# A new order of all five instruction lists in an attention and expert feed-forward kernel

## The chip, the cores and the metric

The kernel runs on one core of one Trainium2 chip. Its time is the device time of one execution in microseconds (us), smaller is better. A core has five engines, each working through its own list of instructions: TensorE (PE; its weight loads are shown as PEld), VectorE (DVE), ScalarE (ACT), GpSimd (POOL) and SyncE (SP), which here only issues transfers. ScalarE issues a few transfers too.

## The reference

For 8 batches of 128 rows and 256 columns, in float32: normalise x, attend over the 256 columns of the context in 8 heads of width 16, add; normalise again, and put each row through one of two experts (256 to 1024 to 256, a squared leaky ReLU between), chosen by a router; add.

```python
def reference(x, ctx_2048, itok_B_779_1933, L0_ffn_w_router, L0_ffn_w_fc, L0_ffn_w_proj):
    x = x + _L0_xcond_ref(_layernorm(x, axis=-1), ctx_2048, ctx_2048, itok_B_779_1933)
    x = x + _L0_ffn_ref(_layernorm(x, axis=-1), L0_ffn_w_router, L0_ffn_w_fc, L0_ffn_w_proj)
    return x
# attention
    s = SCALE * jnp.log(k_length.astype(jnp.float32))[:, None, None, None]
    attn = jnp.einsum('bhdq,bhdk->bhqk', qh, kh)
    attn = jax.nn.softmax(s * attn, axis=-1)
    out = jnp.einsum('bhqk,bhdk->bhdq', attn, vh)
# experts
    h = jnp.einsum('nd,ehd->enh', x_flat, w_fc)
    a = jnp.square(jnp.where(h >= 0, h, 0.5 * h))
    expert_out = jnp.einsum('enh,edh->end', a, w_proj)
    out = jnp.einsum('end,en->nd', expert_out, mask * top_weight[None, :])
```

## The kernel before

Every matmul of the reference is done as a sum of products of high and low parts: a float32 operand is split into a rounded part (`_hi`, a copy on ScalarE into the type fp32r) and the rest (`_lo`, a subtraction on VectorE or GpSimd), and hi*hi, hi*lo and lo*hi are added in PSUM.

The work is cut into 8 batches (b) for the attention and 4 groups of two batches (g) for the feed-forward. Each engine has a list of calls written out by hand; the order of the list is the order of execution on that engine. Between engines, semaphores are counted: a call waits until the counters that it needs have reached a value, and everything behind it on its engine waits with it.

Attention of one batch. x is loaded (`load_x`), its mean and variance are taken (`x_moments`, three stages, VectorE), the inverse root is found on ScalarE (`x_ln`, `x_rstd`) and refined (`x_newton`), and q is normalised (`q_normalise`) and split (`q_part_hi`, `q_part_lo`). The keys are loaded (`load_kv`) and split (`k_part_hi`, `split_k`). Six transfers from SBUF to SBUF spread q and k over the partitions so that the three products lie in one contraction (`stack_q`, `stack_k`, 128 KB each); for q of batch 0 TensorE does it instead (`q_permute`, with the selection `sel` that GpSimd builds from the constants, and `q_put`). `scores_qk(b, g)` computes the scores with queries on partitions, four g per batch, only to find the row maxima (`row_max`, VectorE). The maxima are split (`split_max_hi`, `split_max_lo`), turned (`max_transpose`, TensorE) and copied (`max_rows`, ScalarE). `scores_kq(b, g)` computes the scores with keys on partitions and the maximum taken off; for b below 4 the maximum comes in by extra matmuls with `pick`, for later ones through a stack (`stack_max`, with `clear_max` and `stack_pick` before it). `exp(b, g)` on ScalarE gives the weights, with a scale that needs `len_scale`. `values(b, 0)` and `values(b, 1)` multiply by the values (`load_v`, `place_v`), 16 matmuls of 32 columns each. VectorE turns and divides the result (`pv_turn`, `den_inverse`, `attention_out`, `attention_turn`) and adds x (`keep`, `x2_sum`).

Feed-forward of one group. `x2_moments`, `y_ln`, `y_rstd`, `x2_newton`, `x2_normalise` normalise; `x_transpose(g)` turns both batches on TensorE and `xt_part_hi`, `xt_part_lo` split them. `ffn1(g, c)` is 6 matmuls for 128 hidden units, c from 0 to 15; for two c at a time `leaky` and `square_hi` (ScalarE), `square` (GpSimd) and `square_lo` (VectorE) give the high and low part, and `ffn2(g, c)` is 6 matmuls that add up the output of an expert. `router`, `coef_*`, `coefs` and `expert_out` weight and add, `store` writes. The weights come in 16 pieces of 256 KB (`load_weights(0, n)` for w_fc, `(1, n)` for w_proj), each split by `split_w` on ScalarE and then on GpSimd or, for w_proj, `split_w_lo` on VectorE.

`warm(k)` and `fill(n)` are matmuls of zeros (two matmul records each) that give TensorE something to do.

TensorE works in four shapes: 128 rows by 128 columns (ffn1, ffn2, x_transpose, zeros, max_transpose up to batch 3), 64 rows (both scores), 32 columns (values), and 128 by 32 for max_transpose from batch 4 on.

Two lines set what waits on the maxima and on the scores of a batch:

```python
wait(pe, s_max, PAIRS * b + (g - sets + 1))          # scores_qk: sets = 2 for b < 2, else 1
wait(pe, s_exp, PAIRS * b + g - (1 if b == 1 and g > 0 else 0))   # scores_kq
```

## Time and profile before

| | before |
|---|---|
| median of 3 runs | 173.63 us (172.86 to 173.75) |
| span of the profiled execution | 170.4 us |
| TensorE busy | 161.4 us (95%) |
| VectorE busy | 129.2 us (76%) |
| ScalarE busy | 97.0 us (57%) |
| GpSimd busy | 58.6 us (34%) |
| bytes moved by DMA | 16.98 MB |

The span runs from the first to the last instruction of one profiled execution; the time of a run has what surrounds the program on top. A busy time is an average over stages with different limits, and a matmul's end is modelled, so that TensorE can be shown busy while it runs below its pace: the step from one matmul's start to the next tells more.

### The profile page before, as it was taken

What the parts mean: (1) busy time and instruction counts of PE and PEld (TensorE: products, weight loads), DVE (VectorE), ACT (ScalarE), POOL (GpSimd) and SP (SyncE); (2) the same over time, 40 slices, a digit from 0 to 9 for tenths busy, and PEclk for the clock granted to TensorE, in tenths of its full rate; (3) what the DMA queues carried; (4) which work ended last, traced back from release to release, by engine and by line L of the source; (5) the groups of instructions that cost most, each with busy time, mean ns of one, the idle gap of its engine ahead of it and who ended that gap; (6) DMA issues with size and microseconds to landing.
All of it is one profiled execution on the core that took longest, in us unless ns stands there. A gap on an engine that the chain in (4) does not pass through costs nothing.

```text
span 170.4 us, 4075 instructions
## 1 busy us (share of the span) xinstructions
PE 161.4 (95%) x1494; PEld 139.9 (82%) x1494; DVE 129.2 (76%) x301; ACT 97.0 (57%) x181; POOL 58.6 (34%) x68
## 2 busy tenths in 40 slices
PE   7998887899999989999989999999999999999992
PEld 7986745487698869896978798969879999999991
DVE  7799987999898999995999867953179875056442
ACT  4444979558659956957346526943794065335220
POOL 7331544630322420372521260405023253136330
PEclk9999999999999999999999999999999999999999
DMA  4577857794468054004501460002010000010001
GB/s 120 167 241 246 259 190 233 217 292 126 143 229 251 3 161 120 14 19 139 174 0 62 125 189 4 0 0 67 0 62 0 4 0 0 4 61 0 0 4 62
DMA packets 18883, 16.98 MB, mean 100 GB/s; under 512 B 1776, under 2 KB 18672, under 8 KB 18864
## 3 DMA queue, kind: packets, MB, share of 16 engines
q1 hardware_dynamic: 18144, 16.00, 30.3%
q10 hardware_dynamic: 720, 0.73, 1.5%
q8 instruction: 12, 0.20, 0.5%
q14 instruction: 7, 0.06, 0.1%
HBM read 8.72 MB, written 1.05 MB: 57 GB/s over the span
## 4 chain that ended last, share of the span: by engine, by line
PE 75%; DVE 11%; issue 4%; SPq 3%; ACT 3%; DMA 2%; DVEq 0%; ACTq 0%
PE hp L1358 25%; PE ops L1388 22%; PE pv L1342 6%; PE stp L1318 6%; PE ops L1273 5%; DVE negm L813 5%; PE snp L1265 3%; DMA x_raw<-x 2%; ACT probs L514 2%; DVE a_lo L921 2%; PE ops L1376 2%; PE pv L1376 1%; PE stp L1324 1%; PE pv L1398 1%; PE snp L1301 1%
## 5 line engine op out<-in xcount | busy, mean ns | idle before, releaser
L378 POOL TENSOR_TENSOR a_buf<-l_buf 128x512 f32<-128x512 f32 x32 | 35.7, 1119 | 77.8 <-DVE a_lo L921 44.6
L514 ACT ACTIVATE probs<-stp,scale_b 128x1024 f32<-128x1024 f32 x30 | 33.4, 1114 | 14.8 <-PE stp L1318 11.3
L1358 PE MATMUL hp<-xt_hi,wfc_hi 128*128 128x256 f32 x128 | 37.2, 291 | 0.0
L813 DVE TENSOR_REDUCE negm<-snp 128x4 f32<-128x1024 f32 x28 | 34.1, 1218 | 3.6 <-PE snp L1265 3.4
L1358 PE MATMUL hp<-xt_hi,wfc_lo 128*128 128x256 f32 x128 | 35.8, 279 | 0.0
L1358 PE MATMUL hp<-xt_lo,wfc_hi 128*128 128x256 f32 x128 | 35.7, 279 | 0.0
L522 ACT ACTIVATE l_buf<-hp 128x512 f32<-128x512 f32 x32 | 18.8, 594 | 23.7 <-PE hp L1358 17.0
L921 DVE TENSOR_TENSOR a_lo<-a_buf,a_hi 128x512 fp32r<-128x512 f32 x32 | 26.2, 831 | 7.6 <-ACT a_hi L529 6.2
L1358 PEld LDWEIGHTS hp<-xt_hi,wfc_hi 128*128 128x128 f32 x128 | 24.0, 188 | 2.1 <-issue 1.0
L1388 PE MATMUL ops<-wproj_hi,a_hi 128*128 128x256 f32 x112 | 23.6, 292 | 0.5 <-DVE wproj_lo L953 0.5
L1358 PEld LDWEIGHTS hp<-xt_hi,wfc_lo 128*128 128x128 f32 x128 | 24.1, 188 | 0.0
L1358 PEld LDWEIGHTS hp<-xt_lo,wfc_hi 128*128 128x128 f32 x128 | 24.1, 188 | 0.0
L1388 PE MATMUL ops<-wproj_hi,a_lo 128*128 128x256 f32 x112 | 22.3, 281 | 0.0
L1388 PE MATMUL ops<-wproj_lo,a_hi 128*128 128x256 f32 x112 | 22.3, 281 | 0.0
L529 ACT ACTIVATE a_hi<-l_buf 128x512 fp32r<-128x512 f32 x32 | 19.7, 625 | 2.2 <-PE ops L1388 2.1
L1388 PEld LDWEIGHTS ops<-wproj_hi,a_hi 128*128 128x128 f32 x112 | 17.1, 188 | 2.1 <-issue 1.1
L1273 PE MATMUL ops<-blank 128*128 128x128 f32 x100 | 17.0, 321 | 1.1 <-DVE blank L808 1.1
L1388 PEld LDWEIGHTS ops<-wproj_hi,a_lo 128*128 128x128 f32 x112 | 17.2, 188 | 0.0
L1388 PEld LDWEIGHTS ops<-wproj_lo,a_hi 128*128 128x128 f32 x112 | 17.2, 188 | 0.0
L1318 PE MATMUL stp<-q_st,k_st 64*128 64x256 f32 x120 | 16.1, 319 | 1.0 <-ACT probs L514 0.8
L1273 PEld LDWEIGHTS ops<-blank 128*128 128x128 f32 x100 | 14.7, 224 | 2.7 <-DVE blank L808 1.1
L1342 PE MATMUL pv<-probs,v_one 128*32 128x256 f32 x256 | 16.8, 385 | 0.0
(112 smaller groups left out, 237.2 us busy)
## 6 DMA issues: line engine op xcount, KB each, us to landing
k_st<-k_hi SPq DMA_DIRECT2D x16, 128.0 KB, 2.1
wfc_raw<-w_fc_t SPq DMA_DIRECT2D x8, 256.0 KB, 4.4
wproj_raw<-w_proj_t SPq DMA_DIRECT2D x8, 256.0 KB, 3.5
q_st<-q_hi SPq DMA_DIRECT2D x14, 128.0 KB, 2.1
x_raw<-x SPq DMA_DIRECT2D x8, 128.0 KB, 3.0
k_st<-k_lo SPq DMA_DIRECT2D x8, 128.0 KB, 2.4
v_raw<-ctx_t SPq DMA_DIRECT2D x8, 128.0 KB, 2.6
x_keep<-x SPq DMA_DIRECT2D x8, 128.0 KB, 2.7
```

Of the source, the lines that this page charges most:

```text
L378: pool.tensor_tensor(a_buf[d % 2][:, :, :], l_buf[d % 2][:, :, :], l_buf[d % 2][:, :, :], ALU.mult).then_inc(s_a, 1)
L514: act.activation(probs[g][:, :, :, :], pair[:, :, :].rearrange("p e (c n) -> p e c n", c=KC), ACT.Exp, scale=scale_b[:, b:b + 1]).then_inc ...
L522: act.activation(l_buf[d % 2][:, :, :], hp[:, d % 2, :].rearrange("p (c n) -> p c n", c=2), ACT.Prelu, alpha=0.5).then_inc(s_l, 1)
L529: act.activation(a_hi[d % NA][:, :, :], l_buf[d % 2][:, :, :], ACT.Square).then_inc(s_ahi, 1)
L813: dve.tensor_reduce(negm[b % 2][:, :, :, g].rearrange("p c e -> p e c"), pair[:, :, :].rearrange("p e (c n) -> p e c n", c=KC), AX.X, ALU. ...
L921: dve.tensor_tensor(a_lo[d % NA][:, :, :], a_buf[d % 2][:, :, :], a_hi[d % NA][:, :, :].bitcast(f32), ALU.subtract).then_inc(s_alo, 1)
L1265: last = pe.matmul(pair[:, e, qc * KEYS:(qc + 1) * KEYS], q_st[j][rows, g, qc * P:(qc + 1) * P], k_st[j][rows, g, :], start=(qc == 0), sto ...
L1273: pe.matmul(ops_[:, 0:P], blank[:, :], blank[:, :], start=True, stop=True, skip_group_check=True)
L1318: last = pe.matmul(pair[:, e, kc * DIM:(kc + 1) * DIM], k_st[j][rows, g, kc * P:(kc + 1) * P], q_st[j][rows, g, :], start=(kc == 0), stop= ...
L1342: last = pe.matmul(pv[32 * g:32 * g + 32, e * DIM:(e + 1) * DIM], v_one[j][:, kc * HEADS + h, :], probs[h // 2][:, h % 2, kc, :], start=(e ...
L1358: last = pe.matmul(hp[:, d % 2, half], wfc[w][:, kc, c * P:(c + 1) * P], xt[:, kc, :], start=(c % 2 == 0 and kc == 0 and w == 0 and xt is ...
L1388: last = pe.matmul(ops_[:, t * DIM:(t + 1) * DIM], a[d % NA][:, c % 2, t * P:(t + 1) * P], wproj[w][:, c, :], start=(c % CH == 0 and part ...
```

## The change

All five lists are written in a new order. No call is added or dropped, and no call is changed. On SyncE the first two weight pieces go ahead of the first stacks, and x, keep, v and kv loads and weight pieces are placed between the stacks of one batch and the next instead of among them. On ScalarE the constants are issued ahead of the first keys, and several `split_w` go earlier. On VectorE the moments of x of batches 6 and 7, `x2_normalise` and `q_part_lo` move, as do the low parts of w_proj. On GpSimd `fill_v`, `make_zeros`, `split_k` and `place_v` move. On TensorE the zeros are spread differently, scores and feed-forward calls are interleaved differently, and `values(b, 0)` and `values(b, 1)` are set apart by other calls from batch 2 on. In the core of the diff the heading of each part names the engine's list.

```diff
# SyncE
             load_x(sp, 0)
             load_x(sp, 1)
+            load_weights(sp, 0, 0)
+            load_weights(sp, 0, 1)
             stack_k(sp, 0, 0)
             stack_k(sp, 0, 1)
             stack_k(sp, 0, 2)
+            load_v(1)
             load_x(sp, 2)
-            load_kv(sp, 2)
-            load_weights(sp, 0, 0)
-            load_v(0)
+            load_weights(sp, 0, 2)
+            load_weights(sp, 0, 3)
+            keep(1)
+            load_x(sp, 3)
             stack_k(sp, 1, 0)
             stack_k(sp, 1, 1)
+            stack_k(sp, 1, 2)
             stack_q(sp, 1, 0)
             stack_q(sp, 1, 1)
-            load_x(sp, 3)
-            stack_k(sp, 1, 2)
             stack_q(sp, 1, 2)
-            load_weights(sp, 0, 1)
-            keep(0)
-            load_weights(sp, 0, 2)
-            load_weights(sp, 0, 3)
+            load_v(0)
...
# GpSimd
 
+            fill_v(0)
             zero_k(0)
             zero_k(1)
             zero_nm(0)
             zero_nm(1)
-            fill_v(0)
-            fill_v(1)
-            make_zeros()
             fill_sel(0)
             fill_sel(1)
             split_k(1)
             split_w(0, 0)
+            split_w(0, 1)
+            split_w(0, 2)
             place_v(0)
             split_k(2)
-            split_w(0, 1)
-            split_w(0, 2)
+            fill_v(1)
+            place_v(1)
             split_w(0, 3)
             split_k(3)
-            place_v(1)
+            split_k(4)
             split_w(0, 4)
             split_w(0, 5)
+            place_v(2)
+            place_v(3)
             split_w(0, 6)
-            place_v(2)
             split_w(0, 7)
-            place_v(3)
-            split_k(4)
             square(0, 0)
             square(0, 1)
+            split_k(5)
             square(0, 2)
             square(0, 3)
-            split_k(5)
             square(0, 4)
             square(0, 5)
+            make_zeros()
             place_v(4)
+            place_v(5)
+            split_k(6)
+            split_k(7)
             square(0, 6)
-            split_k(6)
             square(0, 7)
-            place_v(5)
-            split_k(7)
             square(1, 0)
+            square(1, 1)
             place_v(6)
-            square(1, 1)
+            place_v(7)
             square(1, 2)
             square(1, 3)
# ScalarE
 
-            act.preload_act_table_set("natural_log_exp_and_others")
+            act.preload_act_table_set('natural_log_exp_and_others')
+            load_consts()
             load_kv(act, 0)
-            load_consts()
             load_kv(act, 1)
             k_part_hi(0)
             x_ln(0)
             x_rstd(0)
-            q_part_hi(0)
             x_ln(1)
             x_rstd(1)
-            k_part_hi(1)
+            q_part_hi(0)
+            pick_rows()
...
             x_rstd(2)
+            x_ln(3)
+            x_rstd(3)
             exp(0, 0)
-            x_ln(3)
-            split_w(0, 1)
-            x_rstd(3)
             exp(0, 1)
+            k_part_hi(2)
+            k_part_hi(3)
+            exp(0, 2)
+            exp(0, 3)
...
# VectorE
             x_moments(0, 0)
             x_moments(0, 1)
             x_moments(0, 2)
+            len_float()
             split_first_k()
+            x_moments(1, 0)
             x_newton(0, 0)
+            x_moments(1, 1)
             x_newton(0, 1)
+            x_moments(1, 2)
             q_normalise(0)
-            x_moments(1, 0)
-            x_moments(1, 1)
-            x_moments(1, 2)
             q_part_lo(0)
-            len_float()
             x_newton(1, 0)
             x_newton(1, 1)
+            q_normalise(1)
             q_put()
-            q_normalise(1)
+            q_part_lo(1)
             row_max(0, 0)
-            q_part_lo(1)
             row_max(0, 1)
             row_max(0, 2)
             row_max(0, 3)
...
             row_max(1, 3)
-            x_moments(4, 1)
+            x_moments(5, 0)
+            q_part_lo(2)
             split_max_hi(1)
-            q_part_lo(2)
+            x_newton(4, 0)
             split_max_lo(1)
-            x_moments(4, 2)
+            x_newton(4, 1)
+            x_moments(5, 1)
+            x_moments(5, 2)
             pv_turn(0)
...
+            x2_moments(0, 1)
             row_max(2, 1)
-            x2_moments(0, 1)
-            x_moments(6, 0)
             x2_moments(0, 2)
-            x_moments(6, 1)
             row_max(2, 2)
...
             row_max(3, 0)
+            x_newton(5, 1)
+            x2_newton(0, 1)
             x2_newton(1, 0)
+            x2_normalise(0)
             x2_newton(1, 1)
+            row_max(3, 1)
             x2_normalise(1)
-            row_max(3, 1)
-            x_newton(5, 0)
+            q_part_lo(4)
+            row_max(3, 2)
             xt_part_lo(0)
-            x_newton(5, 1)
...
-            router_diff()
+            row_max(3, 3)
+            split_max_hi(3)
+            router(0)
+            split_max_lo(3)
+            split_w_lo(1, 0)
+            x_moments(6, 0)
             q_normalise(5)
-            row_max(3, 2)
-            q_part_lo(4)
...
+            x2_moments(2, 0)
+            split_max_hi(4)
+            split_max_lo(4)
+            square_lo(0, 1)
             x_moments(7, 0)
             x_moments(7, 1)
-            square_lo(0, 0)
...
-            pv_turn(3)
-            q_part_lo(5)
-            coefs(0)
             den_inverse(3)
             attention_out(3)
...
+            x2_normalise(2)
+            x2_normalise(3)
+            split_w_lo(1, 4)
+            coefs(0)
+            row_max(5, 0)
+            square_lo(0, 3)
             q_normalise(6)
...
+            x_newton(7, 0)
             row_max(5, 3)
-            q_normalise(7)
-            router(2)
             split_max_hi(5)
             split_max_lo(5)
+            square_lo(0, 5)
             split_w_lo(1, 5)
             pv_turn(4)
+            den_inverse(4)
+            q_part_lo(6)
+            x_newton(7, 1)
+            split_w_lo(1, 6)
+            split_w_lo(1, 7)
+            router(2)
+            router(3)
             square_lo(0, 6)
-            split_w_lo(1, 6)
             square_lo(0, 7)
-            den_inverse(4)
+            square_lo(1, 0)
             attention_out(4)
-            split_w_lo(1, 7)
-            router(3)
+            row_max(6, 0)
             attention_turn(4)
...
# TensorE
+            warm(12)
             q_permute(0)
-            warm(12)
             q_permute(1)
             warm(13)
...
+            warm(45)
             max_transpose(2)
-            warm(45)
+            scores_kq(2, 0)
+            scores_qk(3, 0)
             warm(46)
             warm(47)
-            scores_kq(2, 0)
-            scores_qk(3, 0)
             fill(2)
             scores_kq(2, 1)
             scores_qk(3, 1)
             warm(48)
-            x_transpose(0)
+            warm(49)
             scores_kq(2, 2)
             scores_qk(3, 2)
-            warm(49)
+            x_transpose(0)
+            scores_kq(2, 3)
+            scores_qk(3, 3)
             ffn1(0, 0)
             ffn1(0, 1)
-            scores_kq(2, 3)
-            scores_qk(3, 3)
-            values(2, 0)
-            values(2, 1)
             ffn1(0, 2)
             ffn1(0, 3)
+            values(2, 0)
+            max_transpose(3)
             ffn1(0, 4)
-            ffn1(0, 5)
-            max_transpose(3)
-            ffn2(0, 0)
+            values(2, 1)
             scores_kq(3, 0)
             scores_qk(4, 0)
+            ffn1(0, 5)
             ffn1(0, 6)
-            ffn2(0, 1)
             scores_kq(3, 1)
             scores_qk(4, 1)
             ffn1(0, 7)
             ffn1(0, 8)
             scores_qk(4, 2)
             scores_kq(3, 2)
+            ffn2(0, 0)
+            ffn2(0, 1)
+            scores_qk(4, 3)
+            scores_kq(3, 3)
+            values(3, 0)
             ffn1(0, 9)
-            ffn1(0, 10)
-            scores_kq(3, 3)
-            scores_qk(4, 3)
-            values(3, 0)
             values(3, 1)
             max_transpose(4)
+            ffn1(0, 10)
             ffn1(0, 11)
             ffn1(0, 12)
...
             ffn1(1, 0)
             ffn1(1, 1)
+            scores_kq(4, 3)
+            scores_qk(5, 3)
+            values(4, 0)
+            ffn2(0, 8)
+            values(4, 1)
+            max_transpose(5)
+            ffn2(0, 9)
             ffn1(1, 2)
             ffn1(1, 3)
-            scores_qk(5, 3)
-            scores_kq(4, 3)
-            ffn2(0, 8)
-            ffn2(0, 9)
...
+            ffn2(1, 8)
+            ffn2(1, 9)
             scores_kq(6, 1)
             scores_qk(7, 1)
-            ffn1(1, 15)
-            ffn2(1, 8)
-            x_transpose(2)
-            ffn2(1, 9)
+            ffn1(2, 0)
+            ffn1(2, 1)
             scores_qk(7, 2)
             scores_kq(6, 2)
-            ffn2(1, 10)
-            ffn1(2, 0)
...
```

## Rows read from the trace of the kernel before

**Rows 1.** The page: its head, and GpSimd's squares (busy us, mean ns | idle).
```profile
span 170.4 us, 4075 instructions
...
L378 POOL TENSOR_TENSOR a_buf<-l_buf 128x512 f32<-128x512 f32 x32 | 35.7, 1119 | 77.8 <-DVE a_lo L921 44.6
```

**Rows 2.** Three stretches: length, busy us of each engine, granted clock, DMA share.
```profile
0.00:41.94 41.94, 37.39 (x340) 29.38 (x341) 36.75 (x94) 26.69 (x56) 17.79 (x28) 1.00 0.68 212
41.94:44.50 2.56, 2.56 (x28) 2.29 (x32) 2.54 (x6) 1.29 (x3) 0.74 (x1) 1.00 0.18 61
44.50:167.12 122.62, 121.46 (x1130) 108.20 (x1130) 89.24 (x201) 68.99 (x124) 40.02 (x39) 1.00 0.21 62
```

**Rows 3.** The chain of waits, 8 to 45 us: start us, us, what.
```profile
15.80 1.12 ACT probs L514
...
27.28 4.06 DMA x_raw<-x
31.36 0.43 DVE xst L744
...
36.02 0.67 PE ops L1273 x6
...
41.94 1.65 PE hp L1358 x12
```

**Rows 4.** Timeline of ScalarE and its queue: start us, us, what [idle before <-releaser].
```profile
0.77 0.66 ACTq L159 DMA_DIRECT2D kv_raw<-ctx_kv  x1
1.47 0.85 ACTq L451 DMA_DIRECT2D cst<-consts  x1
...
3.54 0.42 ACT L470 ACTIVATE k_hi<-kv_raw 128x256 fp32r<-128x256 f32 x1 [1.52 <-DMA kv_raw<-ctx_kv]
...
5.49 0.42 ACT L476 ACTIVATE q_hi<-q_f 128x256 fp32r<-128x256 f32 x1 [0.93 <-DVE q_f L775]
...
7.42 0.60 ACT L456 ACTIVATE q_st<-stp 128x512 fp32r<-128x512 f32 x1 [0.44 <-PE stp L1283]
```

**Rows 5.** Timeline of VectorE, start of the list.
```profile
5.04 0.41 DVE L775 TENSOR_SCALAR q_f<-x_raw,xmv,xsc 128x256 f32<-128x256 f32 x1
```

**Rows 6.** Timeline of TensorE, the first zeros.
```profile
1.06 5.38 PE L1273 MATMUL ops<-blank 128*128 128x128 f32 x24 [1.06 <-DVE blank L808]
```

**Rows 7.** Timeline of TensorE: scores inside a batch, and from ffn2 over scores to ffn1.
```profile
53.27 0.28 PE L1318 MATMUL stp<-q_st,k_st 64*128 64x256 f32 x2
53.38 0.28 PE L1324 MATMUL stp<-mx,pick 64*128 64x256 f32 x2
...
66.15 0.40 PE L1388 MATMUL ops<-wproj_lo,a_hi 128*128 128x256 f32 x2
66.39 0.40 PE L1388 MATMUL ops<-wproj_hi,a_lo 128*128 128x256 f32 x2
66.72 0.50 PE L1265 MATMUL snp<-k_st,q_st 64*128 64x256 f32 x4
...
67.61 0.28 PE L1358 MATMUL hp<-xt_hi,wfc_lo 128*128 128x256 f32 x1
```

**Rows 8.** Timeline of TensorE: the first two matmuls after values.
```profile
128.25 0.39 PE L1358 MATMUL hp<-xt_hi,wfc_hi 128*128 128x256 f32 x1
128.48 0.28 PE L1358 MATMUL hp<-xt_hi,wfc_lo 128*128 128x256 f32 x1
```

**Rows 9.** Timeline of TensorE: three waits [idle before <-releaser].
```profile
27.35 0.50 PE L1265 MATMUL snp<-k_st,q_st 64*128 64x256 f32 x4 [0.69 <-DMA q_st<-q_lo]
...
61.45 0.39 PE L1301 MATMUL snp<-cst,nm_r 128*32 128x128 f32 x2 [0.49 <-DVE nm_r L831]
...
86.47 0.47 PE L1388 MATMUL ops<-wproj_hi,a_hi 128*128 128x256 f32 x2 [0.54 <-DVE wproj_lo L953]
```

**Rows 10.** The page's transfers: count, KB each, median us from issue to landing.
```profile
k_st<-k_hi SPq DMA_DIRECT2D x16, 128.0 KB, 2.1
wfc_raw<-w_fc_t SPq DMA_DIRECT2D x8, 256.0 KB, 4.4
```

621 lines of the change are left out of this document (299 added, 322 removed).

## The prediction

> **What bounds the kernel now.** I read the page's head for the span [rows 1], then three stretches cut where TensorE's list changes character [rows 2], the chain of waits through the first 45 us [rows 3], the start of ScalarE's, VectorE's and TensorE's lists [rows 4 to 6], TensorE's timeline where it goes from one kind of work to another [rows 7, 8], its waits [rows 9] and the time from issue to landing of two kinds of transfer [rows 10].
>
> The span is 170.40 us [rows 1]; the median of the three runs, 173.63, lies 3.2 us above it for what surrounds the program. I add the change of the span to the median.
>
> There are two regimes. Up to 41.94 us, where the feed-forward matmuls begin, TensorE is filled with zeros and waits for a chain: the chain of waits goes through ScalarE's exponentials, VectorE's row maxima and, at 27.28, a 4.06 us wait for the x of batch 6 [rows 3]. From 44.50 to 167.12 TensorE is the bound: 121.46 of 122.62 us busy, 1.16 us idle in all [rows 2]. The granted clock is 1.00 (2.4 GHz) in both. So time can be won by starting the second stretch sooner, or by spending TensorE's time in it better. Removing idle time there can win 1.2 us and no more.
>
> **Part 1: the first 8 us.** ScalarE's list now issues the constants before the first keys (kv of batch 0). Before, the keys were issued at 0.77 and k_part_hi(0) began at 3.54, 2.77 later; the constants' issue came at 1.47 and took 0.85 [rows 4]. The keys would be issued near 1.62 and be used near 4.4. The trace has no case of keys behind constants. Bounds: 3.6 (the constants cost nothing, packets interleave) to 4.9 (a 128 KB load from a busy queue); I take 4.4, since it is the same load with the same 2.77. Behind it on ScalarE stands x_ln(0), so the scale of x is late by the same 0.9. VectorE's list also puts x_moments(1) between x_newton's steps, so q_f, which began at 5.04 [rows 5], begins near 6.2; q_hi moves from 5.49 to about 6.65, as x_ln(1) and x_rstd(1) are now ahead of it, and the ScalarE half of q_put from 7.42 [rows 4] to about 8.1. VectorE gives 0.3 back: q_part_lo(1) no longer stands between the first row maxima. I get the first batch's maxima 0.4 us late. The constants' own gain (sel is ready earlier) is hidden, since q_hi is then the later of the two.
>
> **Part 2: from there to the feed-forward.** exp(0,0), before at 15.80 [rows 3], is later by 0.5: beside the 0.4, x_moments(3) stands ahead of len_scale on VectorE. The four exponentials of batch 0 and the scores between them are a closed loop and keep that lag. Before split_max_lo(1) come x_moments(5,0) and q_part_lo(2), some 0.75 us by rows such as 31.36's 0.43 [rows 3], so batch 1's maxima are about 1 us late. Then the lag is won back. Before, VectorE stood behind x of batch 6, which its list read at 31.36 after a 4.06 us transfer [rows 3]; the new list reads it after row_max(3,3), some 13 us later. And scores_kq(2,0) no longer waits behind the three zeros that took 0.67 at 36.02 [rows 3]: it goes 0.3 us earlier than before. Nothing is late at that point. But then x2_normalise(1) goes behind row_max(3,1), and x_transpose(0) and xt_part_lo(0) behind row_max(3,2). By VectorE's order xt_lo is ready near 43.3, so ffn1(0,0) begins near 43.4 and not 41.94 [rows 3]. It then has scores_kq(2,3) and scores_qk(3,3) behind it, which before ended at 44.50 with two ffn1 also done [rows 2]. Two ffn1 are 12 matmuls of 0.118 (0.24 for two, from 66.15 to 66.39 [rows 7]), 1.4 with 0.1 for the switch below. 43.4 + 1.5 is 44.9 against 44.50: **+0.4 us** for the whole head. SyncE's order (weight pieces, x, keep and v moved past the stacks) costs nothing here as long as a stack lands when the maxima need it. For batch 2 the three k stacks now go first and the q stacks last; with 2.1 to land [rows 10] I count the last there near 27.6, and VectorE is ready for it at 28.3.
>
> **Part 3: waits in the dense part.** At 61.45 TensorE waited 0.49 for the split maxima of batch 4, at 86.47 0.54 for the last low part of the projection weights [rows 9]. In the new order VectorE has both over a microsecond ahead of TensorE's need: split_w_lo(1,7) stands ahead of router(2), and the maxima of batch 4 come earlier because x of batch 7 and coefs(0) moved behind them. I followed the queues through the list (each operation by its own row of the kernel before, such as 1.12 for an exponential [rows 3] and for a square on GpSimd [rows 1]) and found no new wait above 0.1; the narrowest margins are 0.3 to 0.5 us, at row_max(6,0), row_max(7,1) and x_transpose(3). GpSimd is blocked by split_k(4), place_v(3) and place_v(7), with its squares behind them, but TensorE's reader of those comes later each time. **-1.2 us**, all of the idle time; bounds -1.2 and +1.0 (two new waits like the old ones).
>
> **Part 4: what the dense part does with its time.** Within ffn1 and ffn2 a matmul follows the last in 0.118. Between the last pair of ffn2(0,5) at 66.39 and the second matmul of ffn1(0,14) at 67.61 lie 1.22 us [rows 7]. At full pace this is 0.235 for the pair, eight 64-row matmuls at 0.06 (0.11 for two, 53.27 to 53.38) and 0.118: 0.82. So a visit to the scores costs 0.4 us beyond its matmuls, 0.2 for each change of kind. Values (32-column tiles) show the same exit: the first matmul after them takes 0.23, from 128.25 to 128.48 [rows 8], and not 0.118. Now count the changes of kind (128x128, scores, values, narrow max_transpose) along TensorE's list: from ffn1(0,0) there were 55, two of them before 44.50, and there are 66. The new order sets ffn1, ffn2 or scores between values(b,0) and values(b,1) of every batch from 2 on, which before stood together or had only a transpose between them. That is 13 more at 0.15 (a values entry costs less) to 0.2: **+2.3 us**, bounds 1.3 (0.1 each, the exit alone) and 2.6. Nothing covers it, as no other engine is late there.
>
> The Trainium skill, page "TensorEngine Tiling (Array Packing)", Key Properties, says that changing the tiling mode drains the engine. By that rule alone, which gives no figure, each of the 13 costs something and the change cannot be free; the trace agrees, with about 0.2 us per change between scores and ffn. Had switches been free, the sum would be -0.8 and the forecast would turn round.
>
> **Sum.** +0.4 - 1.2 + 2.3 = +1.5: a span of 171.9 and a time of 173.63 + 1.5 = 175.1 us.
>
> **Rivals.**
> (a) Faster. A switch hides in the loading ahead of weights and costs 0.1 or less in the new places (+1.2), and the head comes out 1.4 us better than mine, 0.8 because the keys land by 3.6 and 0.6 because no stack waits for a weight piece, as at 27.35 where TensorE waited 0.69 for q_st [rows 9]. -1.0 - 1.2 + 1.2 = -1.0: 172.6. For it: the idle times that go are real, and the DMA waits of the head too. Against: the 1.22 at 66.39 is in an ordinary place with nothing else late. It decides from a switch price under 0.1.
> (b) No change that can be told. Switches at 0.15 (+1.9) and a head 1 us better than mine because the first keys land early: -0.6 - 1.2 + 1.9 = +0.1: 173.7.
> (c) Slower still: the first stacks. load_weights(0,0) and (0,1), 512 KB, now stand on SyncE's queue right ahead of the stacks of batch 0. A wfc piece lands 4.4 us after issue, a k_st stack 2.1 [rows 10]. Issued near 2.1 and 2.7, the pieces end near 7; the last stack, issued near 6.3, is needed by 8.7. If it waits for them and takes 1.5 us longer, every maximum of batch 0 is later by about 1.1: 176.2. It decides if a stack behind a weight piece takes more than 2.4 us.
> (d) The change does not do what it says and the clock falls. My walk through the list still has TensorE idle for 0.4 to 0.55 us at q_permute, max_transpose(0), scores_kq(0,3) and max_transpose(1), where zeros ran or not. The longest wait before, 0.69, left the clock at 1.00 [rows 2, 9]. The first 24 zeros took 5.38 us [rows 6], 0.22 each, against 0.11 for the six at 36.02 [rows 3]: at 1.2 GHz all that TensorE does takes twice as long. A slow stretch as long as that first one does 2.7 us of work in 5.4; part of it lies beside waits in the head, so about +2: 177. The Trainium skill, "TensorE: Matmul & The Clock Gate", has the clock fall after idle time; the trace agrees only in its start and shows no fall between.
>
> **How the numbers follow.** A measurement of this kernel can tell about 0.5% (0.9 us) from no change: faster is under 172.8, slower above 174.5. Forecast 0.40, (c) 0.13, (d) 0.04; a quarter for (b) and what lies within the bound; (a) 0.18. Slower 0.57, same 0.25, faster 0.18. The range reaches from (a) to (d)'s edge, 172.6 to 177.0: the bounds of the switches give -1.0 and +0.3 around 175.1, those of the keys' landing -0.8 and +0.5, new waits up to +2.2, and (a) lies at the lower end.
>
> **What would show it.** Right: ffn1(0,0) near 43.4 with scores_qk(3,3) ahead of it; k_part_hi(0) near 4.4; no idle time of TensorE over 0.2 us after 44; the last ffn2 ending near 168.6; values in single groups of 16 with 0.23 for the first matmul after each. Wrong: ffn1(0,0) before 42.5, or a dense stretch that is not longer although switched more often (the price is not per switch), or idle rows on TensorE that name GpSimd or VectorE (my walk missed a wait).

## The result and the profile after

The changed kernel is slower: 173.90 us (median of 20 executions) against 172.73 us for the kernel before (20 executions beside it), a ratio of 1.0064 with a 95% interval of 1.0048 to 1.0081. That is 0.8 to 1.4 us. The forecast was slower by 1.5 us on 173.63, a ratio of 1.0085. The 173.63 was the median of the first three executions; with 20 it is 172.73, so 0.9 of the 1.2 us between the forecast time and the measured one lies in the base and 0.3 in the change. The spans alone tell the same: the median is 172.0 us in the 20 executions of the changed kernel and 170.8 in 71 executions of the kernel before that ran beside the experiments.

| | before | after |
|---|---|---|
| profiled execution, us | not on record | 173.89 |
| its span, us | 170.4 | 172.1 |
| ffn1(0, 0) begins | 41.94 | 44.58 |
| last ffn2 ends | 167.12 | 168.84 |

The page of the changed kernel, its span, the granted clock and the chain that ended last:

```profile
span 172.1 us, 4075 instructions
...
PEclk9999999999999999999999999999999999999999
...
PE 76%; DMA 9%; issue 3%; SPq 3%; POOL 3%; ACT 3%; DVE 2%; DVEq 0%; POOLq 0%
```

The same three stretches as [rows 2], of the changed kernel (length, busy us of each engine, granted clock, DMA share, GB/s):

```profile
0.00:41.94 41.94, 36.42 (x332) 28.89 (x334) 36.44 (x90) 26.48 (x55) 15.22 (x25) 1.00 0.72 221
41.94:44.50 2.56, 1.96 (x24) 1.38 (x20) 2.39 (x5) 1.60 (x2) 1.62 (x3) 1.00 0.07 21
44.50:167.12 122.62, 122.00 (x1129) 108.48 (x1130) 88.63 (x206) 68.80 (x124) 40.15 (x42) 1.00 0.20 60
```

In the third stretch TensorE is idle for 0.62 us where it was idle for 1.16 [rows 2], so waits did go. It is busy for longer all the same, and it starts later, as the waits in the second stretch show. TensorE's timeline there (start us, us, engine line operation tile, count, [idle before <-releaser]):

```profile
42.27 0.66 PE L1398 MATMUL pv<-cst,x2n 128*128 128x128 f32 x4
43.31 0.39 PE L1318 MATMUL stp<-q_st,k_st 64*128 64x256 f32 x2 [0.39 <-ACT probs L514]
...
43.89 0.40 PE L1265 MATMUL snp<-k_st,q_st 64*128 64x256 f32 x4
44.58 0.36 PE L1358 MATMUL hp<-xt_hi,wfc_hi 128*128 128x256 f32 x1 [0.28 <-issue]
```

x_transpose(0) runs at 42.27, behind scores_qk(3, 2), and ffn1(0, 0) comes last, at 44.58. Before, ffn1(0, 0) began at 41.94 [rows 3] and filled the wait for the third exponential with two ffn1 calls. After 44.58 the trace has one wait, and it is none of the three in [rows 9]:

```profile
83.22 0.50 PE L1318 MATMUL stp<-q_st,k_st 64*128 64x256 f32 x4 [0.54 <-DMA q_st<-mx]
```

scores_kq(5, 0) waits for the stacked maxima of batch 5.

**Two measures for all that follows.** The *end of the head* is where all scores of batches 2 and 3 up to scores_qk(3, 3) are done and no ffn1 is: in the new order the start of ffn1(0, 0), in the old order the start of scores_qk(3, 3) plus its 0.40, less 1.41 for the two ffn1 calls already done. The *dense part* is the time from there to the end of the last ffn2. In the two profiles the head ends at 43.09 and 44.58 and the dense part takes 124.03 and 124.26 us. So 1.5 of the 1.7 us between the spans lie in the head. A single profile can mislead here, as the kernels below show: those that leave one head as it is are further samples of that head.

### The profile page after: what moved, and what is told of

It reads as the page before. It is cut to its first block, busy times and chain, and to the rows that moved or that the text cites. A ratio compares the mean times of both kernels' runs of the same rounds, so it can differ in the third digit from the quotient of the medians.

```text
span 172.1 us, 4075 instructions
## 1 busy us (share of the span) xinstructions
PE 162.1 (94%) x1494; PEld 140.3 (82%) x1494; DVE 128.3 (75%) x301; ACT 96.9 (56%) x181; POOL 57.0 (33%) x68
## 3 DMA queue, kind: packets, MB, share of 16 engines
HBM read 8.72 MB, written 1.05 MB: 57 GB/s over the span
## 4 chain that ended last, share of the span: by engine, by line
PE 76%; DMA 9%; issue 3%; SPq 3%; POOL 3%; ACT 3%; DVE 2%; DVEq 0%; POOLq 0%
PE hp L1358 26%; PE ops L1388 24%; PE pv L1342 8%; PE stp L1318 5%; PE snp L1265 5%; DMA wfc_raw<-w_fc_t 4%; DMA q_st<-mx 2%; DMA kv_raw<-ctx_kv 2%; PE ops L1376 2%; PE ops L1273 2%; SPq L176 2%; POOL wfc_lo L371 1%; PE pv L1376 1%; DVE negm L813 1%; ACT probs L514 1%
## 5 line engine op out<-in xcount | busy, mean ns | idle before, releaser
L378 POOL TENSOR_TENSOR a_buf<-l_buf 128x512 f32<-128x512 f32 x32 | 35.1, 1104 | 74.6 <-DVE a_lo L921 46.0
L921 DVE TENSOR_TENSOR a_lo<-a_buf,a_hi 128x512 fp32r<-128x512 f32 x32 | 25.5, 813 | 8.3 <-POOL a_buf L378 4.8
L1318 PE MATMUL stp<-q_st,k_st 64*128 64x256 f32 x120 | 15.5, 309 | 2.9 <-ACT mx L503 1.3
```

The costliest lines, as they stand in the source:

```text
L378: pool.tensor_tensor(a_buf[d % 2][:, :, :], l_buf[d % 2][:, :, :], l_buf[d % 2][:, :, :], ALU.mult).then_inc(s_a, 1)
L921: dve.tensor_tensor(a_lo[d % NA][:, :, :], a_buf[d % 2][:, :, :], a_hi[d % NA][:, :, :].bitcast(f32), ALU.subtract).then_inc(s_alo, 1)
L1318: last = pe.matmul(pair[:, e, kc * DIM:(kc + 1) * DIM], k_st[j][rows, g, kc * P:(kc + 1) * P], q_st[j][rows, g, :], start=(kc == 0), stop= ...
```

## The experiments

**1 and 2. Each head with the other dense part.** All five lists are cut where scores_qk(3, 3) is done and the rest goes in the other kernel's order. TensorE's list at the joint, first old head with new dense part, then the mirror image:

```diff
 scores_qk(3, 3)
-values(2, 0)
-values(2, 1)
 ffn1(0, 2)
 ffn1(0, 3)
-ffn1(0, 4)
-ffn1(0, 5)
+values(2, 0)
 max_transpose(3)
+ffn1(0, 4)
+values(2, 1)
...
```

> All five lists follow the kernel before as far as its work of the first 44.4 us goes (up to scores_qk(3, 3) on TensorE, 92 calls), and from there the order of the changed kernel. Theory A (the prediction's sum: head +0.4, dense part +2.3 for changes of kind and -1.2 for waits): 1.1 us slower than the kernel before. Theory B (the changed kernel's profile: ffn1(0, 0) at 44.58, where the prediction had 43.4, and an end 1.72 us later; head about +1.5, dense part about +0.2): within 0.4 us of the kernel before, and faster than the changed kernel by 1.0 to 1.5.

```diff
 scores_qk(3, 3)
 ffn1(0, 0)
 ffn1(0, 1)
+values(2, 0)
+values(2, 1)
 ffn1(0, 2)
 ffn1(0, 3)
-values(2, 0)
-max_transpose(3)
 ffn1(0, 4)
...
```

> The mirror image: all five lists follow the changed kernel up to scores_qk(3, 3) on TensorE (90 calls), and from there the order of the kernel before. Theory A: 0.4 us slower than the kernel before. Theory B: 1.0 to 1.5 us slower, so that nearly all of the change's loss is here and its dense part costs next to nothing.

Measured: ratios of 1.0186 (1.0149 to 1.0222) and 1.0136 (1.0109 to 1.0162) to the kernel before, 3.2 and 2.4 us slower. Both theories missed. The joint itself costs more than either half. TensorE in the first of the two:

```profile
52.48 0.78 PE L1265 MATMUL snp<-k_st,q_st 64*128 64x256 f32 x4 [1.89 <-DMA q_st<-q_lo]
53.19 0.58 PE L1358 MATMUL hp<-xt_hi,wfc_hi 128*128 128x256 f32 x1
...
54.63 0.41 PE L1358 MATMUL hp<-xt_hi,wfc_hi 128*128 128x256 f32 x1
```

and its windows, with the granted clock in the last column but two:

```profile
44.50:51.00 6.50, 6.08 (x72) 4.30 (x70) 5.26 (x13) 5.13 (x10) 2.14 (x3) 1.00 0.65 206
51.00:57.00 6.00, 4.52 (x29) 3.96 (x29) 3.14 (x6) 2.04 (x4) 2.08 (x3) 0.72 0.53 172
```

SyncE issued the first stack of batch 4 at 47.06, where the changed kernel has it at 44.14, since loads stood ahead of it at the joint. scores_qk(4, 0) then waited 1.89 us, and behind that wait the clock was at its lower level (1.2 GHz) for some 3.5 us: ffn1(0, 5) took 1.44 from its start to that of ffn1(0, 6), where 0.81 is usual behind scores. From there on every call lies 2.9 to 3.0 us behind the changed kernel, to the end. The mirror image waited 0.65 for an exponential at 48.80 and 0.43 for maxima at 53.33. So the two do not tell head from dense part by their times, but their halves are samples of the two heads.

**3. The price of a change of kind, alone.** One ffn1 call goes between values(b, 0) and values(b, 1) in four batches of the kernel before (the counts in the expectations take x_transpose and max_transpose(3) as kinds of their own; the prediction's 55 and 66 did not; both give 11 more, 13 with the two ahead of 44.50):

```diff
-values(2, 1)
 ffn1(0, 2)
+values(2, 1)
...
 values(5, 0)
+ffn1(1, 10)
 values(5, 1)
 max_transpose(6)
-ffn1(1, 10)
...
```

> The kernel before with one ffn1 call moved between values(b, 0) and values(b, 1) for b = 2, 5, 6 and 7: 8 changes of kind more on TensorE (62 to 70 from ffn1(0, 0) on), nothing else. Theory A (0.15 to 0.2 us for each change, whatever the kinds): 1.2 to 1.6 us slower. Theory B (the price belongs to the neighbours: two values calls behind scores take 1.05 and 0.99 in the kernel before, two single ones in the changed kernel 1.00 each, so that a split costs only the 0.09 and 0.1 of the ffn calls at its edges): 3 x 0.16 + 0.32 = 0.8 us slower.

Measured: 1.0069 (1.0043 to 1.0095), 1.2 us slower. The dense part takes 125.17 us, 1.14 more than 124.03. Of this, scores_qk(7, 0) has a new wait, which puts it 0.42 behind its neighbours' usual pace:

```profile
104.86 0.50 PE L1265 MATMUL snp<-k_st,q_st 64*128 64x256 f32 x4 [0.34 <-DMA q_st<-q_lo]
```

What is left is 0.7 us for eight changes, 0.09 each: theory B. TensorE at the first of the four places, and below it the same place of the kernel before:

```profile
45.65 1.07 PE L1342 MATMUL pv<-probs,v_one 128*32 128x256 f32 x16
46.65 0.39 PE L1358 MATMUL hp<-xt_hi,wfc_hi 128*128 128x256 f32 x1
46.87 0.28 PE L1358 MATMUL hp<-xt_hi,wfc_lo 128*128 128x256 f32 x1
...
47.55 1.07 PE L1342 MATMUL pv<-probs,v_one 128*32 128x256 f32 x16
48.55 0.39 PE L1358 MATMUL hp<-xt_hi,wfc_hi 128*128 128x256 f32 x1
```

```profile
44.43 2.11 PE L1342 MATMUL pv<-probs,v_one 128*32 128x256 f32 x32
46.47 0.39 PE L1358 MATMUL hp<-xt_hi,wfc_hi 128*128 128x256 f32 x1
```

Two values calls side by side take 2.04 from 44.43 to 46.47; apart they take 1.00 each (45.65 to 46.65, 47.55 to 48.55). Here being apart costs the values calls nothing. Only the ffn1 call between them pays: 0.90 from 46.65 to 47.55, where 0.705 is its pace within ffn1; 0.11 of it is the first matmul behind values, 0.09 the last one ahead of them.

**4. The new dense order with the pairs put back together.**

```diff
 values(2, 0)
+values(2, 1)
 max_transpose(3)
 ffn1(0, 4)
-values(2, 1)
...
```

> The changed kernel with values(b, 0) and values(b, 1) set side by side again for b = 2 to 7: 6 changes of kind fewer (73 to 67), nothing else. Theory A (0.15 to 0.2 us for each): 0.9 to 1.2 us faster than the changed kernel. Theory B (summed by the rows of each neighbourhood: -0.11, -0.11, -0.07, +0.04, +0.04, -0.12): 0.3 us faster than the changed kernel, so still slower than the kernel before by 0.7 to 1.0.

Measured: 1.0092 (1.0060 to 1.0125) to the kernel before, so no faster than the changed kernel's 1.0064, and theory A's 0.9 to 1.2 us are excluded. (Three of the seven executions take 2.7 to 3.1 us more than their span, the others 1.8 to 2.0; the median span is 171.7 us, and 172.0 for the changed kernel.) The profile's dense part is 123.75 us, 0.5 less than 124.26, and the wait ahead of scores_kq(5, 0) is shorter by as much (0.10 beyond the usual pace, and not 0.62). But the edit brought a wait of its own: values(7, 0) no longer stands ahead of scores_kq(7, 3), which now waits for an exponential. The first row is one of the pairs, the second that wait:

```profile
47.61 1.93 PE L1342 MATMUL pv<-probs,v_one 128*32 128x256 f32 x32
...
126.87 0.50 PE L1318 MATMUL stp<-q_st,k_st 64*128 64x256 f32 x4 [0.31 <-ACT probs L514]
```

From the start of ffn2(1, 15) ahead of it to ffn1(2, 10) behind it this takes 1.85, where the usual pace is 1.34, so 0.51 is waiting. Without the waits the dense part is 123.14 us here and 123.64 in the changed kernel: the six changes are worth 0.5 us, 0.08 each, between theory B's 0.3 and theory A. All of it is on the values side, since as many ffn visits are left: five of the six pairs now take 1.87 (47.61 to 49.48 for the first), where two single calls take 2.00.

**5 to 7. The first 25 us of the new head.** First the keys alone put back ahead of the constants:

```diff
-load_consts()
 load_kv(act, 0)
+load_consts()
```

> The changed kernel with one swap on ScalarE: the keys of batch 0 are issued ahead of the constants again. In three profiles of the changed kernel's head k_part_hi(0) began at 4.21, 4.39 and 4.47, in three of the old head at 3.54, 3.60 and 3.77. Theory A (the prediction: the lag of the first 8 us is carried by the loop of exponentials): k_part_hi(0) near 3.6, scores_qk(0, 0) 0.6 earlier at 8.1, SyncE's stacks 0.65 earlier too since its queue issues without a pause from 4.65 on, and the whole kernel 0.6 us faster than the changed one. Theory C (batch 1's stacks, held up by weight pieces, set scores_qk(1, 0) at 17.95 to 19.02 and with it scores_kq(0, 1)): scores_kq(0, 1) moves by less than 0.3, and the time by less than 0.3.

Measured: 1.0133 (1.0096 to 1.0171), 1.2 us slower than the changed kernel and not 0.6 faster. Both theories missed. The keys did come first, k_part_hi(0) at 3.58, but VectorE shows what then waited:

```profile
5.71 0.17 DVE L786 CAST len_f<-cst 128x8 f32<-128x8 int32 x1 [1.61 <-DMA cst<-consts]
...
7.07 0.41 DVE L775 TENSOR_SCALAR q_f<-x_raw,xmv,xsc 128x256 f32<-128x256 f32 x1
```

and TensorE, and the granted clock of the stretch:

```profile
8.08 0.72 PE L1283 MATMUL stp<-q_hi,a_hi 128*128 128x256 f32 x4 [1.83 <-ACT q_hi L476]
8.63 0.96 PE L1283 MATMUL stp<-q_lo,a_lo 128*128 128x256 f32 x4
```

```profile
5.50:12.30 6.80, 4.97 (x29) 4.15 (x27) 5.01 (x15) 3.61 (x10) 2.82 (x4) 0.75 0.70 203
```

The constants landed at 5.69, behind the two weight pieces that the change puts at the front, and VectorE's len_float, early in its new list, holds x_newton and q_normalise(0) for them. So the new place of the constants belongs to the new place of the weights and of len_float: one of the three cannot be undone alone. Second, the weight pieces behind batch 1's stacks:

```diff
-load_weights(sp, 0, 2)
-load_weights(sp, 0, 3)
-keep(1)
 load_x(sp, 3)
...
 stack_q(sp, 1, 2)
+load_weights(sp, 0, 2)
+load_weights(sp, 0, 3)
+keep(1)
```

> The changed kernel with the weight pieces w_fc 2 and 3 and the kept x of batch 1 issued on SyncE behind the six stacks of batch 1 instead of ahead of them, and their splitting moved behind exp(0, 1) and exp(0, 2) on ScalarE and behind place_v(1) on GpSimd. Theory C (the weight pieces hold up the stacks of batch 1 on the queue, and their splitting holds up max_rows(0) on ScalarE): last stack of batch 1 landing at 14 to 15.5 and not 17.9, max_rows(0) 0.4 to 0.8 earlier, scores_kq(0, 1) at 17.4 to 17.7 and not 18.3 to 19.4, and 0.6 to 1.0 us faster than the changed kernel. Theory A (the stacks cost nothing as the lag comes from the first keys and is won back by batch 3): scores_kq(0, 1) no more than 0.3 earlier, time within 0.3 us of the changed kernel.

Measured: 1.0040 (1.0019 to 1.0061), 0.4 us faster than the changed kernel by the medians of the ratios, with intervals that overlap. The mechanism is there. The transfers issued in the first 20 us (KB each, median us from issue to landing), of the changed kernel and then of this one:

```profile
q_st<-q_hi SPq DMA_DIRECT2D x2, 128.0 KB, 3.3
...
q_st<-q_lo SPq DMA_DIRECT2D x1, 128.0 KB, 3.9
```

```profile
q_st<-q_hi SPq DMA_DIRECT2D x2, 128.0 KB, 2.4
...
q_st<-q_lo SPq DMA_DIRECT2D x1, 128.0 KB, 2.1
```

In these two profiles a q stack of batch 1 behind two weight pieces takes 3.3 to 3.9 us to land, one without them 2.1 to 2.5, and the k stacks ahead of them 4.2 to 4.8 and 2.6 to 2.8. TensorE of the changed kernel waits for the last of them, with scores_kq(0, 1) and the loop of exponentials behind it; with the pieces behind the stacks scores_qk(1, 0) ran at 17.26 without a wait:

```profile
17.95 0.51 PE L1265 MATMUL snp<-k_st,q_st 64*128 64x256 f32 x4 [0.40 <-DMA q_st<-q_lo]
```

The Trainium skill, "DMA: Bandwidth & Descriptors", section "Two DMAs through the same engine are not ordered", says that within one queue of one DMA engine descriptors start in order; the landing times above agree, but do not show that the order, and not the amount in flight, is the reason. The second effect is on ScalarE of the changed kernel:

```profile
14.39 1.24 ACT L542 ACTIVATE wfc_hi<-wfc_raw 128x512 fp32r<-128x512 f32 x2 [4.05 <-DMA wfc_raw<-w_fc_t]
15.53 0.36 ACT L503 ACTIVATE mx<-pv 128x256 fp32r<-128x256 f32 x1
```

max_rows(0) stands behind two splits of weights that have just landed; without them it began at 15.28. Third, everything of the start put back together:

```diff
+load_kv(act, 0)
 load_consts()
-load_kv(act, 0)
...
-load_weights(sp, 0, 0)
-load_weights(sp, 0, 1)
...
 stack_k(sp, 0, 2)
+load_weights(sp, 0, 0)
+load_weights(sp, 0, 1)
...
-len_float()
...
 q_part_lo(0)
+len_float()
```

> The changed kernel with its first 20 us put back in four places together: the keys of batch 0 ahead of the constants on ScalarE, the weight pieces w_fc 0 and 1 behind batch 0's three stacks on SyncE, w_fc 2, 3 and the kept x of batch 1 behind batch 1's six stacks (with their splitting as in the run with the weights behind), and len_float behind q_part_lo(0) on VectorE. With the keys alone put first, the constants landed at 5.69 behind the weight pieces, and len_float, which stands early in VectorE's list and reads them, held q_normalise(0) to 7.07. Theory C (weight pieces ahead of everything are what made constants, stacks and maxima late): q_permute near 6.2, scores_kq(0, 1) near 17.0, max_transpose(1) about 1.3 earlier than the changed kernel's 25.3 to 26.4, and 0.7 to 1.2 us faster than the changed kernel. Theory H (the hole is at 38 to 44.6, in the order of x2_normalise(1), xt_part_lo(0) and ffn1(0, 0)): what is won by 25 us is lost again before 44, and the time is within 0.3 us of the changed kernel.

Measured: 1.0047 (1.0022 to 1.0071). The keys (k_part_hi(0) at 3.65) add nothing to what the weight pieces gave. scores_kq(0, 1) is at 17.49 and not 18.30, but max_transpose(1) is at 25.43 where the changed kernel has 25.34: it waits 0.8 us for VectorE, whose new list has x_moments(5, 0) and q_part_lo(2) ahead of split_max_lo(1). The next link, scores_qk(2, 0), began at 27.94, 0.04 after the last stack of batch 2 had landed and without idle time: VectorE and the stacks were due together there.

**8 and 9. The last steps ahead of the feed-forward.** In the changed kernel, ffn1 brought forward:

```diff
+x_transpose(0)
 scores_kq(2, 2)
 scores_qk(3, 2)
-x_transpose(0)
+ffn1(0, 0)
+ffn1(0, 1)
 scores_kq(2, 3)
 scores_qk(3, 3)
-ffn1(0, 0)
-ffn1(0, 1)
```

> The changed kernel with x2_normalise(0) and (1) and xt_part_lo(0) earlier on VectorE (ahead of and right behind row_max(3, 1)), xt_part_hi(0) ahead of exp(2, 2) on ScalarE, and on TensorE x_transpose(0) ahead of scores_kq(2, 2) and ffn1(0, 0), (0, 1) ahead of scores_kq(2, 3), as the kernel before had them. Theory H: ffn1(0, 0) near 43, scores_qk(3, 3) ending near 45.4 with two ffn1 done, and 0.5 us faster than the changed kernel. Theory C: TensorE has waited for the exponentials of batch 2 anyway, whose lag comes from earlier, and the time is within 0.2 us of the changed kernel.

Measured: 1.0064 (1.0042 to 1.0087), as the changed kernel. ffn1(0, 0) came at 42.63, but it waited 0.92 us for xt_hi, so that the head, counted as for the other kernels, ends 7.2 us after scores_kq(2, 0), no sooner than in the new order. Another wait came eight microseconds on, ahead of scores_qk(4, 0):

```profile
42.63 0.36 PE L1358 MATMUL hp<-xt_hi,wfc_hi 128*128 128x256 f32 x1 [0.92 <-ACT xt_hi L538]
...
51.02 0.50 PE L1265 MATMUL snp<-k_st,q_st 64*128 64x256 f32 x4 [0.38 <-DMA q_st<-q_lo]
```

That left open whether the order of these steps costs anything, so the reverse was made in the kernel before, this part of the change alone:

```diff
-x_transpose(0)
 scores_kq(2, 2)
 scores_qk(3, 2)
+x_transpose(0)
-ffn1(0, 0)
-ffn1(0, 1)
 scores_kq(2, 3)
 scores_qk(3, 3)
+ffn1(0, 0)
+ffn1(0, 1)
```

with x2_normalise(0) behind row_max(3, 0), x2_normalise(1) behind row_max(3, 1), xt_part_lo(0) behind row_max(3, 2) and xt_part_hi(0) behind exp(2, 2).

> The kernel before with one part of the change alone, the order of the last steps ahead of the feed-forward: on VectorE x2_normalise(0) behind row_max(3, 0), x2_normalise(1) behind row_max(3, 1) and xt_part_lo(0) behind row_max(3, 2), on ScalarE xt_part_hi(0) behind exp(2, 2), on TensorE x_transpose(0) behind scores_qk(3, 2) and ffn1(0, 0), (0, 1) behind scores_qk(3, 3). In four profiles of the old head the last scores and two ffn1 calls were done, counted back by 1.41 for these two, 6.5 us after scores_kq(2, 0) began; in four of the new head ffn1(0, 0) began 7.1 to 7.4 us after it. Theory H (this order is what the head lost behind batch 2's first scores): ffn1(0, 0) 7.1 to 7.4 us after scores_kq(2, 0), and 0.6 to 0.9 us slower than the kernel before. Theory C (the late stacks of batches 1 and 3 are the cause): within 0.3 us of the kernel before.

Measured: 1.0061 (1.0034 to 1.0088), 1.05 us slower. TensorE:

```profile
42.60 0.39 PE L1318 MATMUL stp<-q_st,k_st 64*128 64x256 f32 x2 [0.17 <-ACT probs L514]
...
43.44 0.50 PE L1265 MATMUL snp<-k_st,q_st 64*128 64x256 f32 x4
44.08 0.36 PE L1358 MATMUL hp<-xt_hi,wfc_hi 128*128 128x256 f32 x1
```

scores_kq(2, 0) began at 36.75 and ffn1(0, 0) 7.33 later: theory H. (The profile's dense part is longer too, by 0.47 us, with waits ahead of scores_qk(6, 0) and scores_qk(7, 0).) Nine profiles of the two orders, us (starts; end of the head as defined above):

| kernel | scores_kq(2, 0) | end of head | between |
|---|---|---|---|
| old head: before | 36.62 | 43.09 | 6.47 |
| before_values_apart | 37.85 | 44.31 | 6.46 |
| before_waits_out | 37.78 | 44.24 | 6.46 |
| head_before_dense_after | 37.37 | 43.82 | 6.45 |
| new head: after | 37.17 | 44.58 | 7.41 |
| after_values_together | 37.50 | 44.64 | 7.14 |
| after_kq5_later | 36.95 | 44.17 | 7.22 |
| head_after_dense_before | 38.15 | 45.51 | 7.36 |
| old head, this part new: before_ffn1_late | 36.75 | 44.08 | 7.33 |

Up to scores_kq(2, 0), before_ffn1_late is a fifth sample of the old head, and after_ffn1_early (36.61) one of the new. The kernel before was profiled in the execution with the earliest scores_kq(2, 0) of these five. Taken as means both heads get there at the same time, 37.27 and 37.28, though single profiles lie up to 1.5 us apart. The stretch behind it takes 6.46 in the old order and 7.28 in the new: there lie the 0.82 us by which the new head ends later.

Ahead of it the means hide a loss and a gain. In all fifteen profiles scores_qk(2, 0) begins 0.04 to 0.05 us after the last stack of batch 2 has landed, and the first of these stacks is issued 0.1 us after scores_kq(0, 3) ends. In the changed kernel (the kernel before is at 27.35, [rows 9]):

```profile
28.50 0.51 PE L1265 MATMUL snp<-k_st,q_st 64*128 64x256 f32 x4 [0.58 <-DMA q_st<-q_lo]
```

On the means of the same five profiles each, scores_qk(2, 0) begins at 28.61 in the new head and 27.70 in the old, so 0.9 later: what the first batches lose arrives here. From there scores_kq(2, 0) follows 8.67 later in the new head and 9.57 in the old one, so the 0.9 is won back and no more.

**10. The one new wait.**

```diff
+ffn2(0, 10)
 scores_kq(5, 0)
-ffn2(0, 10)
```

> The changed kernel with ffn2(0, 10) moved ahead of scores_kq(5, 0) on TensorE. In four profiles of the new dense order scores_kq(5, 0) waited for the stacked maxima of batch 5 to land, beyond its neighbours' pace by 0.44 to 0.68 us. Theory (the only wait left in the new dense part, and nothing is due right behind it): that wait goes, the stretch from ffn1(0, 0) to the last ffn2 is 123.7 us long and not 124.2, and the time 0.4 to 0.5 us less than the changed kernel's. Rival: scores_kq(5, 1) then waits for exp(5, 0), the stretch keeps its length.

Measured: 1.0076 (1.0044 to 1.0108), which cannot be told from the changed kernel. The profile shows the rival in part: the wait for the stacked maxima is gone, and the next scores wait for the exponential.

```profile
82.95 0.50 PE L1318 MATMUL stp<-q_st,k_st 64*128 64x256 f32 x4
...
84.67 0.50 PE L1318 MATMUL stp<-q_st,k_st 64*128 64x256 f32 x4 [0.31 <-ACT probs L514]
```

The dense part takes 124.06 us, 0.2 less.

**11 to 13. The change's two gains taken without its price.** x of batch 6 read later in the kernel before:

```diff
 row_max(2, 1)
-x_moments(6, 0)
...
 row_max(3, 3)
+x_moments(6, 0)
+x_moments(6, 1)
+x_moments(6, 2)
```

> The kernel before with x_moments(6, *) moved on VectorE from between row_max(2, 1) and row_max(2, 2) to behind row_max(3, 3), and what follows from them (x_ln, x_rstd, x_newton of batch 6) moved behind them. Three profiles of the old head show VectorE waiting 0.33, 0.83 and 1.00 us there for x of batch 6, and ffn1(0, 0) at 41.94, 42.69 and 43.17 with it. Theory B (that one wait sets where the second stretch starts and scatters the times): 0.5 to 1.1 us faster than the kernel before, ffn1(0, 0) near 41.5, and a smaller scatter. Rival (another step is due at the same point, so the time lies idle elsewhere): within 0.3 us of the kernel before.

Measured: 0.9983 (0.9966 to 1.0000), 0.3 us faster, less than either end of the expectation's 0.5 to 1.1. The head did gain: scores_kq(2, 0) at 36.15, against a mean of 37.27, and its end at 42.61. Why the old head scatters is seen on VectorE, at its first step with x of batch 6, here in before_values_apart:

```profile
32.60 0.43 DVE L744 BATCH_NORM_STATS2 xst<-x_raw 128x6 f32<-128x256 f32 x1 [1.00 <-DMA x_raw<-x]
```

In the kernel before's own profile this wait is 0.33 ahead of the 31.36 in [rows 3]. In all five profiles of the old head scores_kq(2, 0) begins 5.25 to 5.26 us after the start of this step, so the landing of that x sets it. In before_x6_later TensorE then waited for the last stack of batch 6, 0.45 ahead of scores_qk(6, 0) at 85.69, so part of the gain was lost again. Next, the waits in the dense part, by VectorE's list alone:

```diff
-split_w_lo(1, 2)
 row_max(4, 3)
...
 split_max_lo(4)
+split_w_lo(1, 2)
...
 split_w_lo(1, 5)
+split_w_lo(1, 6)
+split_w_lo(1, 7)
 pv_turn(4)
```

> The kernel before with three operations moved on VectorE alone: split_w_lo(1, 2) behind split_max_lo(4), and split_w_lo(1, 6) and (1, 7) into the 1.7 us in which VectorE waits ahead of pv_turn(4). TensorE's list is unchanged, so it has no change of kind more. Theory A of the waits (all three idle times of TensorE go: 0.49 at 61.45, 0.54 at 86.47, 0.2 at 88.25): 1.0 to 1.2 us faster than the kernel before. Rival (the next wait stands right behind and takes their place): less than 0.5 us faster.

Measured: 0.9958 (0.9940 to 0.9976), 0.7 us faster, between theory and rival. The three waits are gone; scores_qk(6, 0) is 0.25 behind its usual pace instead. And both together, with keep(4) behind stack_q(6, 2):

```diff
-keep(4)
 stack_q(sp, 6, 2)
+keep(4)
```

> The kernel before with the moves of two earlier runs together, and one more: x_moments(6, *) behind row_max(3, 3) (alone 0.3 us faster), split_w_lo(1, 2), (1, 6) and (1, 7) moved on VectorE (alone 0.8 us faster), and keep(4) behind stack_q(6, 2) on SyncE, since the last stack of batch 6 landed at 85.65 and 86.37 there and scores_qk(6, 0) waited for it. TensorE's list is that of the kernel before. If the three add up: 1.2 to 1.5 us faster than the kernel before, near 171.3. If what one wins the next wait takes: 0.8 us faster.

Measured: 170.97 us, 0.9884 (0.9866 to 0.9902), 2.0 us faster than the kernel before, more than the 1.2 to 1.5 expected, and 3 us faster than the changed one. It is the fastest of all. Its windows, cut as [rows 2] where its own ffn1(0, 0), values(2, 0) and last ffn2 lie:

```profile
0.00:41.88 41.88, 37.66 (x341) 29.74 (x341) 36.33 (x91) 26.54 (x54) 17.82 (x28) 1.00 0.66 213
41.88:44.43 2.55, 2.55 (x28) 2.28 (x32) 2.45 (x6) 1.20 (x3) 0.74 (x1) 1.00 0.18 57
44.43:165.75 121.32, 121.32 (x1130) 108.22 (x1130) 89.62 (x204) 69.37 (x126) 39.45 (x39) 1.00 0.21 63
```

TensorE is busy for all of the last 121.32 us. TensorE's list is unchanged here, so a dense part without idle time was to be had without a single change of kind more.

## Why the prediction was right or wrong

The direction and the kinds of term were right: waits go, changes of kind come, the head is late, and the sum is a loss of about 1 us. Each of the three terms was off, and the errors partly cancel. The step that failed by most is the price of a change of kind: "13 more at 0.15 (a values entry costs less) to 0.2", +2.3 us with 1.3 as the lower bound, where the runs show about 1.0, 0.07 each. Rival (a) named a price of 0.1 or less and was right in that; its other half, a head 1.4 us better, did not come.

- **The base.** The sum stood on 173.63; the kernel before takes 172.73. That was bad luck: of the first three executions two (173.63 and 173.75) are the longest of all 91 of this kernel, and why is not shown. The profile errs the other way. The wait for x of batch 6 (0.33 to 1.00 us in five profiles) scatters the spans, and the profiled one had the earliest scores_kq(2, 0) of five; its span is 170.4 where the median of 71 is 170.8.
- **The head, forecast +0.4, measured about +0.8.** The step that failed is "the lag is won back", which put scores_kq(2, 0) 0.3 earlier than before; between the means it is 0.0. The x of batch 6 did give its share: the old head with it read later has scores_kq(2, 0) at 36.15 and 36.55, against 37.27. (What VectorE itself waits for is 0.33 us here; the 4.06 of [rows 3], which the prediction calls a wait, is the length of the transfer.) The new order's first part cost as much again, some 0.9 us, where the forecast left 0.3 of the gain over. Experiment 9 shows it in the landing of batch 2's stacks: the prediction had the last of them landing near 27.6 and VectorE ready at 28.3, and scores_qk(2, 0) began at 28.61 on the mean. Part of this is rival (c)'s mechanism, one batch later than the prediction put it: batch 0's stacks took 2.5 to 2.7 us, over the 2.4 that (c) names, but landed by 8.57 and scores_qk(0, 0) began at 8.70, when the prediction needed it; batch 1's landed as late as 17.91. With the pieces behind them scores_kq(2, 0) is at 37.01 and 36.75, against 37.28, so 0.3 to 0.5 us, as far as two profiles can tell. The prediction dismissed this with a sentence, that SyncE's order "costs nothing here", and followed the landing of batch 2's stacks through the new queue, not of batch 1's. The other step, from scores_kq(2, 0) to ffn1(0, 0), was right: 36.3 to 43.4 is 7.1, measured 7.14 to 7.41, and experiment 9 shows that this order alone makes the stretch 0.9 us longer than the old order's 6.46.
- **The keys.** Forecast 4.4 for k_part_hi(0), measured 4.05 to 4.47 in the five profiles in which the first 20 us were left as they are. What they cost the total cannot be told from nothing: putting them back along with the weights gave no more than the weights alone.
- **The waits, forecast -1.2, measured about -0.9.** The old waits are worth 1.3 us: before_three_moves has them out, and its dense part is 122.73 us where the kernel before has 124.03. The new order did remove them, and brought one back: scores_kq(5, 0) is 0.62, 0.48, 0.44 and 0.14 behind its usual pace in four profiles of this dense part, 0.42 on the mean. The step that failed is "no new wait above 0.1".
- **The changes of kind, forecast +2.3, measured about +1.0.** Without the wait at scores_kq(5, 0) the new dense part takes 123.64 to 123.73 us in four profiles (124.26 - 0.62, 124.19 - 0.48, 124.13 - 0.44, 123.87 - 0.14), the old one without waits 122.73. That is some 0.95 for 13 changes, 0.07 each, below the lower bound of 0.1; experiments 3 and 4 give 0.09 and 0.08. Summed call by call against before_three_moves, with its wait taken off, the changed kernel's ffn calls take 0.86 us more (29 visits to them for 23), its scores 0.25 more, its values 0.04 less and its transposes 0.2 less. The price of 0.2 was read off a visit to scores [rows 7], where it holds, and carried over to values, which are what the change moved. The 0.23 for the first matmul behind values [rows 8] is the price for the ffn side, 0.11 above the pace, and the last matmul ahead of them costs 0.09. The values side costs nothing where the pair took 2.04, as four of the six did in before_three_moves, and 0.13 for a pair that takes 1.87, as in experiment 4. The Trainium skill, "TensorEngine Tiling (Array Packing)", Key Properties, says that a change of tiling mode drains the engine; the trace agrees that changes cost time, and shows that how much depends on the two kinds, from 0.07 each on the average of the 13 here to 0.2 around scores.

With the measured terms the sum is +0.8 - 0.9 + 1.0 = +0.9, and the interval of the measured ratio gives 0.8 to 1.4. Of the signs named beforehand, the values do stand in single groups of 16 with 0.23 for the first matmul after, k_part_hi(0) was near 4.4, and the last ffn2 ended at 168.84, near 168.6; ffn1(0, 0) was 1.2 us late, and one wait over 0.2 is there after 44. That the change was forecast within 0.3 us in spite of this is the cancelling of errors: a head too early, waits too well removed, changes of kind too dear.

What stays open: the other 0.4 to 0.6 us that the new order's first batches cost (the later start of batch 0, and VectorE's order ahead of split_max_lo(1), seen to hold max_transpose(1) in experiment 7, were not tried by themselves), and whether the changed kernel with all of its head put right would beat the kernel before; it was tried in parts only.

## What to carry to other kernels

Read the price of a change of kind from the pair of kinds that is moved, from both sides of it, and not from the costliest pair in the trace. Before summing against one profile, ask which of its waits end in a transfer: such a wait has another length in the next execution, so the profiled span may lie at an edge; and a median of three may too, as the 0.9 us in the base show. A stall is often cheapest to remove in the list of the engine that causes it (here three moves on VectorE and one on SyncE): that leaves the order of the bounding engine, and what it has to pay, as it was.
